# Quadratic scores of whole query rows per key block, and a new written order of steps, in a fused attention and expert layer

## What is computed

```python
A = einsum('bchf,bshf->bhcs', q_phi, k_phi) * causal       # quadratic scores, 16 heads
y = einsum('bhcs,bshd->bchd', A, v) / (sum_s A + eps)      # "lin"
win = softmax(q k^T / sqrt(8), 64 keys back) v             # "win"
x = x + concat(lin, win) @ Wout
# expert layer: logits -> top 2 of 8 experts per token, MLP and KAN experts,
# rows gathered by token index, results scatter-added
```

## Time and profile before

| what | value |
|---|---|
| median of 3 runs | 970.09 us (969.99 to 971.36) |
| the profiled execution | 976.52 us |
| its span, first to last instruction | 974.8 us |
| mean granted TensorE clock | 0.919 of full speed |
| TensorE busy | 804.0 us (82%) |
| ScalarE busy | 535.5 us (55%) |
| GpSimd busy | 486.0 us (50%) |
| VectorE busy | 445.0 us (46%) |

### The profile page before, as it was taken

How to read it: one execution, slowest core, us unless ns; L and a number is a source line. 1 busy time by engine, 2 the same in 40 slices (tenths; PEclk the granted TensorE clock), 3 DMA queues, 4 the chain that set the end, 5 groups by cost and what they waited for, 6 DMA issues and landing times.

```text
span 974.8 us, 22796 instructions
## 1 busy us (share of the span) xinstructions
PE 804.0 (82%) x8242; PEld 610.2 (63%) x8243; DVE 445.0 (46%) x1114; ACT 535.5 (55%) x729; POOL 486.0 (50%) x657
## 2 busy tenths in 40 slices
PE   4688877867878878789785696699999999999980
PEld 2456545645655555566562474589788878987870
DVE  7525314315235243254431266347666864767250
ACT  4476645635646646467462345266676766677230
POOL 8232534443346245452446255576577777654532
PEclk9799987987989989899897598799999999999985
DMA  2312130220220401204022514253564454354123
GB/s 64 103 35 62 34 95 2 68 62 1 68 62 2 128 2 52 77 2 128 1 69 55 131 34 95 82 127 53 130 142 101 83 137 121 56 133 67 18 20 103
DMA packets 91059, 68.20 MB, mean 70 GB/s; under 512 B 42894, under 2 KB 83276, under 8 KB 89038
## 3 DMA queue, kind: packets, MB, share of 16 engines
q1 hardware_dynamic: 74014, 55.11, 19.9%
q0 software_dynamic: 16912, 11.35, 8.7%
HBM read 46.86 MB, written 21.37 MB: 70 GB/s over the span
## 4 chain that ended last, share of the span: by engine, by line
PE 58%; issue 11%; POOL 11%; ACT 8%; DVE 5%; another core or an unknown queue 4%; DMA 1%; DVEq 0%; POOLq 0%; ACTq 0%
PE pv L1562 12%; PE ring L1528 10%; PE pv L1663 10%; PE ring L1510 3%; PE ring L1497 3%; PE ring L1589 3%; ACT Pb L954 3%; PE ring L1630 2%; PE ring L1447 2%; PE ring L1616 2%; PE ring L1722 2%; PE ring L1607 2%; ACT Pb L938 2%; POOL c L693 2%
## 5 line engine op out<-in xcount | busy, mean ns | idle before, releaser
L765 POOL DMA_INDIRECT acc_d<-stack,srec x84 | 137.0, 1630 | 63.6 <-DVE stack L1126 32.2
L1663 PE MATMUL pv<-Pb,vaug 128*32 128x128 f32 (+3 forms) x2816 | 138.0, 322 | 25.1 <-issue 24.3
L1204 DVE TENSOR_REDUCE maxima<-ring 128x8 f32<-128x1024 f32 x64 | 78.4, 1225 | 162.5 <-PE ring L1589 133.6
L793 POOL TENSOR_SCALAR_AFFINE_SELECT Pb<-Pb 128x1024 f32<-128x1024 f32 x64 | 68.9, 1093 | 156.3 <-ACT Pb L938 148.7
L944 ACT ACTIVATE Pb<-ring 128x768 f32<-128x768 f32 x128 | 99.6, 812 | 77.9 <-PE ring L1616 69.5
L1138 DVE SCALAR_TENSOR_TENSOR stack<-stack 128x512 f32<-128x512 f32 x160 | 104.3, 691 | 71.0 <-ACT stack L917 55.0
L1663 PEld LDWEIGHTS pv<-Pb,vaug 128*32 128x32 f32 x2816 | 82.8, 110 | 70.6 <-issue 56.3
L1528 PE MATMUL ring<-stack 128*128 128x256 f32 x560 | 124.1, 381 | 0.0
L1528 PEld LDWEIGHTS ring<-stack 128*128 128x128 f32 x560 | 105.4, 190 | 18.5 <-issue 4.7
L822 POOL DMA_INDIRECT slot_d<-rec,pos x64 | 62.4, 975 | 96.6 <-DVE pos L1305 79.5
L917 ACT ACTIVATE stack<-ring,kprm 128x512 f32<-128x512 f32 x160 | 108.2, 814 | 0.1
(11 more groups left out here) (246 smaller groups left out, 1297.0 us busy)
## 6 DMA issues: line engine op xcount, KB each, us to landing
stack<-L_ffn_kan_sl_W SPq DMA_DIRECT2D x20, 1024.0 KB
stack<-hl_d SPq DMA_DIRECT2D x24, 256.0 KB
stack<-hl_d SPq DMA_DIRECT2D x24, 128.0 KB
stack<-L_ffn_mlp_W SPq DMA_DIRECT2D x12, 256.0 KB
hl_d<-hi SPq DMA_DIRECT2D x7, 384.0 KB, 2.6
hl_d<-lo SPq DMA_DIRECT2D x7, 384.0 KB, 4.0
Pb<-L_ffn_mlp_W SPq DMA_DIRECT2D x10, 256.0 KB
xb<-L_attn_x SPq DMA_DIRECT2D x9, 256.0 KB
```

The costliest lines, as they stand in the source:

```text
L765: pool.indirect_dma_start(acc_d, bass.IndirectOffsetOnAxis(ap=srec[:, kind, u % RECS, q, 0:1], axis=0), src[:, u % 2, q, :], None, compute ...
L1204: dve.tensor_reduce(maxima[:, c, 2 * HG * n:2 * HG * (n + 1)].rearrange("p (k j) -> p k j", j=HG), slot(job).rearrange("p k (j q) -> p k j ...
L1663: mm = pe.matmul(pv[32 * j:32 * (j + 1), n // 2 % 2, q0:q0 + w], vaug[:, p, c, head(n, j) // 2, 16 * (n % 2):16 * (n % 2) + 32], src[:, j, ...
```

## The change

Scores: a pass is now 5 jobs of 1024 columns. Job 0 takes key block 2 of all four heads (256 query columns each). Jobs 1 to 4 take one head each: key block 0 with all 512 query columns, block 1 with 384, block 3 with 128. The diagonal blocks thus lie inside longer rows. GpSimd's select becomes four of 512 columns with strides (one after job 0, one after job 2, two after job 4), and the product's wait counts all four. The product takes each key block in one group: 4 groups of 4 matmuls, of 512, 384, 256 and 128 columns. Window scores are as before.

Order: the string `ORDER` is replaced. The front's statistics and coefficients come at the batch's start, `q`, `k`, `u` and `stacks` in its first third, `weights` and with it the scatter's data earlier, `mT` after `store` instead of before, `*egather` after the scatter instead of before.

```diff
--- before.py
+++ after.py
@@ -72,16 +72,16 @@
 ORDER = """
-M L L M -ytr L L M L -ycT L M -out L L L M -coef2 L L +stats M +aggr P +coef L L L L M L M L -h2norm P L +hT
--h2T L -logit L +q L +k mT L L -store P L *eload -choose W W W +u +v -rank P -total W *egather +stacks
-+residual W -gapexp W W P W Y W W -weights +xload P W W W W W W P -scatter P
+L L +stats +aggr +coef -ytr L M L L M -ycT M M -out L -coef2 +hT L M +q L +k L +u L -h2norm M P L +stacks L L L
+P L -h2T M L M -store L -logit mT L L L P -choose -rank -gapexp W W W P -weights -total +residual W W Y W W P
+*eload W W W W P W W W W +xload P -scatter W *egather +v P
 """.split()
 
 
 def batch_steps(u, tail, front):
 
 
-    series = {"L": iter([("lin", n, j, u) for n in range(NHG) for j in range(6)]),
+    series = {"L": iter([("lin", n, j, u) for n in range(NHG) for j in range(5)]),
               "M": iter([("max", n, j, u) for n in range(NHG // 2) for j in range(NT)]),
               "W": iter([("win", n, j, u) for n in range(NHG, 2 * NHG) for j in range(NT)]),
               "P": iter([("pv", n, 0, u) for n in range(2 * NHG)]),
@@ -782,16 +782,25 @@
                     if c < 5:
                         pool.wait_ge(k_cf, tile_no(k, 6, c + 1))
 
+            def own_blocks(pd):
+
+                pool.affine_select(pd, pd, [[0, HG], [1, P]], ALU.is_ge, 0.0, base=0,
+                                   channel_multiplier=-1).then_inc(pd_ready, 1)
+
             def batches():
                 for s, n, j, b in PROGRAM:
-                    if s == "lin" and j < 2:
+                    if s == "lin" and j in (0, 2, 4):
                         job = JOBS[(s, n, j, b)]
                         pool.wait_ge(freed[job % SLOTS], fill_no(job))
                         pool.sem_inc(pool_at, 1)
 
-                        pd = Pb[:, n % 2, 1024 * j:1024 * (j + 1)].rearrange("p (a q) -> p a q", q=P)
-                        pool.affine_select(pd, pd, [[0, 8], [1, P]], ALU.is_ge, 0.0, base=0,
-                                           channel_multiplier=-1).then_inc(pd_ready, 1)
+                        if j == 0:
+                            own_blocks(Pb[:, n % 2, 4 * 1024:5 * 1024].rearrange("p (j q) -> p j q", j=HG)[:, :, 0:P])
+                        else:
+                            own_blocks(Pb[:, n % 2, 1024 * (j - 2):1024 * j].rearrange(
+                                "p (j q) -> p j q", j=HG)[:, :, 0:P])
+                        if j == 4:
+                            own_blocks(Pb[:, n % 2, 0:4 * 1024].rearrange("p (j q) -> p j q", j=HG)[:, :, 1024 - P:])
                     if s == "coef":
                         front_coefficients(b + 1)
                         normed()
@@ -929,21 +938,15 @@
                         act.activation(mT16[:], slot(job)[0:H, 0, :], ACT.Copy, scale=-1.0).then_inc(mT_ready, 1)
                         act.wait_ge(mT_ready, batch_no(b, 1, 1))
                         act.sem_inc(freed[job % SLOTS], 1)
-                    if s == "lin" and j < 2:
+                    if s == "lin":
                         job = JOBS[(s, n, j, b)]
                         wait_filled(act, job)
                         if j == 0:
 
                             act.wait_ge(pv_done, batch_no(b, 8, LEAD + max(n - 1, 0)))
-                        act.activation(Pb[:, n % 2, 1024 * j:1024 * (j + 1)].rearrange("p (k q) -> p k q", k=2),
+                        at = 1024 * (j - 1 if j else HG)
+                        act.activation(Pb[:, n % 2, at:at + 1024].rearrange("p (k q) -> p k q", k=2),
                                        slot(job), ACT.Square, bias=1.0).then_inc(freed[job % SLOTS], 1)
-                    if s == "lin" and j >= 2:
-                        hd = j - 2
-                        job = JOBS[(s, n, j, b)]
-                        wait_filled(act, job)
-                        act.activation(Pb[:, n % 2, 2048 + 768 * hd:2048 + 768 * (hd + 1)].rearrange(
-                            "p (k q) -> p k q", k=2), slot(job)[:, :, 0:384], ACT.Square,
-                            bias=1.0).then_inc(freed[job % SLOTS], 1)
                     if s == "win":
                         c = j
                         job = JOBS[(s, n, c, b)]
@@ -1598,24 +1601,15 @@
                         for c in range(NT):
                             mm = pe.transpose(slot(job)[0:H, 0, P * c:P * (c + 1)], maxima[:, c, :], identf[:])
                         mm.then_inc(filled[job % SLOTS], 1)
-                    if s == "lin" and j < 2:
+                    if s == "lin":
                         job = JOBS[(s, n, j, b)]
                         wait_freed(pe, job)
-                        for bk in range(2):
-                            c = 2 * j + bk
-                            for hd in range(HG):
-                                mm = pe.matmul(slot(job)[:, bk, P * hd:P * (hd + 1)],
-                                               sk[:, head(n, hd), P * c:P * (c + 1)],
-                                               su[:, head(n, hd), P * c:P * (c + 1)], start=True, stop=True)
-                        mm.then_inc(filled[job % SLOTS], 1)
-                    if s == "lin" and j >= 2:
-                        job = JOBS[(s, n, j, b)]
-                        wait_freed(pe, job)
-                        for bk, o, c in ((0, 0, 0), (1, 0, 1), (1, 256, 2)):
-                            w = T - P * (c + 1)
-                            mm = pe.matmul(slot(job)[:, bk, o:o + w],
-                                           sk[:, head(n, j - 2), P * c:P * (c + 1)],
-                                           su[:, head(n, j - 2), P * (c + 1):T], start=True, stop=True)
+                        parts = ([(hd, 2, hd // 2, 2 * P * (hd % 2)) for hd in range(HG)] if j == 0 else
+                                 [(j - 1, 0, 0, 0), (j - 1, 1, 1, 0), (j - 1, 3, 1, T - P)])
+                        for hd, c, bk, o in parts:
+                            w = T - P * c
+                            mm = pe.matmul(slot(job)[:, bk, o:o + w], sk[:, head(n, hd), P * c:P * (c + 1)],
+                                           su[:, head(n, hd), P * c:T], start=True, stop=True)
                         mm.then_inc(filled[job % SLOTS], 1)
                     if s == "win":
                         if n == NHG and j == 0:
@@ -1634,9 +1628,9 @@
                     if s == "pv":
 
                         if n < NHG:
-                            pe.wait_ge(pd_ready, batch_no(b, 8, 2 * n + 2))
-
-                            po_job = JOBS[("lin", n, 5, b)]
+                            pe.wait_ge(pd_ready, batch_no(b, 16, 4 * n + 4))
+
+                            po_job = JOBS[("lin", n, 4, b)]
                             pe.wait_ge(freed[po_job % SLOTS], fill_no(po_job))
                         else:
 
@@ -1645,25 +1639,20 @@
                         if n % 2 == 0:
                             pe.wait_ge(y_out[n // 2 % 2], batch_no(b, 2, LEAD + n // 4))
                         for c in range(NT):
-                            parts = []
                             if n < NHG:
-                                pd = Pb[:, n % 2, 512 * c:512 * (c + 1)].rearrange("p (j q) -> p j q", j=HG)
-                                po = Pb[:, n % 2, 2048:5120].rearrange("p (j q) -> p j q", j=HG)
-                                parts.append((P * c, P, pd))
-                                if c < NT - 1:
-                                    o = (0, 384, 640)[c]
-                                    w = T - P * (c + 1)
-                                    parts.append((P * (c + 1), w, po[:, :, o:o + w]))
+                                w = T - P * c
+                                src = (Pb[:, n % 2, 4 * 1024:5 * 1024] if c == 2 else
+                                       Pb[:, n % 2, 0:4 * 1024]).rearrange("p (j q) -> p j q", j=HG)
+                                o = (0, T, 0, 1024 - P)[c]
                             else:
-                                wq = WQ if c < NT - 1 else P
-                                pw = Pb[:, n % 2, 768 * c:768 * (c + 1)].rearrange("p (j q) -> p j q", j=HG)
-                                parts.append((P * c, wq, pw[:, :, 0:wq]))
-                            for x_, (q0, w, src) in enumerate(parts):
-                                for j in range(HG):
-                                    mm = pe.matmul(pv[32 * j:32 * (j + 1), n // 2 % 2, q0:q0 + w],
-                                                   vaug[:, p, c, head(n, j) // 2, 16 * (n % 2):16 * (n % 2) + 32],
-                                                   src[:, j, :], start=(n % 2 == 0 and c == 0 and x_ == 0), stop=(c == NT - 1),
-                                                   skip_group_check=True)
+                                w = WQ if c < NT - 1 else P
+                                src = Pb[:, n % 2, 768 * c:768 * (c + 1)].rearrange("p (j q) -> p j q", j=HG)
+                                o = 0
+                            for j in range(HG):
```

(4 more changed lines are left out.)

## The result

| | before | after |
|---|---|---|
| median | 970.73 us (969.99 to 972.31, 4 runs) | 932.58 us (927.93 to 940.73, 4 runs) |
| span of the profiled execution | 974.8 us | 938.9 us |
| mean granted TensorE clock | 0.919 | 0.923 |
| TensorE busy | 804.0 us | 790.3 us |

The ratio is 0.9622, 95% interval 0.9586 to 0.9657: 38 us less, where I had forecast 14.5 less and a range down to 939. The profiled executions (976.5 and 940.7 us) both lie above their medians; spans are compared with spans.

The account below looks back on a forecast made before the run. TensorE was taken to bound each batch up to pv7, with the scatter stretch the largest loss. Terms -2.2 - 2.4 - 4.8 + 1.4 + 3.5 - 6 - 4 = -14.5 us gave 956 us from 970.1, range 939 to 977.

Parts of the forecast that it names:

- merging and hand-overs: Scores and product: wider matmuls save 2.2 us over 32 passes, one slot hand-over less per pass saves 2.4 us.
- `hT` for `hn`: TensorE's 0.79 us wait for GpSimd's normalised rows in six batches goes, as coefficients start with the batch: -4.8 us.
- opening of the batch: From pv7 to `out`, 1.4 us of idle instead of 1.2, as `ytr` stands behind fewer score jobs: +1.4 us.
- mixing of the jobs (at nothing): New alternation of score jobs with other jobs: given no term of its own in the sum, so 0 us.
- `mT` behind the stores: On SyncE's queue `mT` travels behind 0.77 MB of stores and win4.0 waits for it: +0.5 x 7 = +3.5 us.
- scatter: Scatter starts 8 to 10 us earlier, its instruction shortage falling on less dense window jobs: -1 x 6 = -6 us.
- last batch: Gather, scatter and second gather run without GpSimd's 5.28 us break and start earlier: -4 us (-9 to +8).
- Order, the front: Moved start-of-batch jobs: -4.8 us for the `hn` wait, +1.4 us for the opening; `q`, `k`, `u` alternate with score jobs.
- It is made up by the product behind them: `q`, `k`, `u` alternating with score jobs take ScalarE 0.92 + 0.6, TensorE 0.43 + 0.9 us; no net charge.
- The 81 ns rule: About 81 ns per 128-column matmul, not 56: 16 diagonal matmuls would save 13 us, giving 945; 2 in 100.
- rival (1): Scatter hits working engines, so pauses of about 7 us strike more often: slower, at about 977 us; 16 in 100.
- (4): Scatter's shortage overlaps ScalarE's backlog (-24 not -6) without pauses, or last batch yields 9: 938 to 946 us; 22 in 100.

## Why the prediction was wrong

The direction was right; the forecast of 956 us was 23 us too slow. Most of the gain lies in a term that I had as small waits taken away one by one, and the saving that I had put on the scatter did not come.

| step | predicted, us | measured |
|---|---|---|
| merging and hand-overs | -4.6 | -2.17 a batch under the new order (six: -12.4), +1.0 at full clock under the old |
| `hT` for `hn` | -4.8 | the wait is gone (0.78 a batch); with the new scores the early coefficients are worth 2.4 a batch, 5.2 with the clock |
| opening of the batch | +1.4 | no cost: pv7 to `out` 8.80 for 9.65, with 8.80 - 8.05 = 0.75 us of idle where I had found 1.4 |
| mixing of the jobs (at nothing) | 0 | the whole order is -3.5 a batch with the old scores (six: -20.5), 0.8 of it `hn` |
| `mT` behind the stores | +3.5 | 0.0 (48.26 against 48.27) |
| scatter | -6 | no saving: 11.5 for 11.0 a batch, within what single traces differ; 1.5 a batch dearer early than late on the other kind of chip |
| last batch | -4 | -0.9 |

- **The step that failed** is "Order, the front". I read 4.7 us of small waits in the earlier trace rows and took away only 0.8 a batch for `hn` and 0.3 for a hand-over. I looked at each moved word for what it adds and not at what its new place does to the jobs around it: a projection between two score jobs is also 0.9 us in which ScalarE catches up. "It is made up by the product behind them" had it as a cost that is repaid; it was part of the gain. What the runs showed in its place: TensorE's waits for ScalarE fall from 3.5 to 1.3 us a batch with the order alone and to 0.5 with the merge, and the order takes 3.5 us off the period with the old scores, 6.7 with the new. The clean period fell by 5.7 us, of which my terms without scatter and last batch (-4.5 us over the kernel) hold 0.6.
- **The merge** was priced right for TensorE's columns: a pass of scores is 1.06 + 2 x 0.82 = 2.70 us before and 0.61 + 2 x 1.04 = 2.69 after, and the product of all four blocks takes 2.36 us in 32 records (16 matmuls) against 2.38 in 56 (28 matmuls). What it saves comes with one job, one slot and one square less, and only where TensorE doesn't wait for something else. I had 0.57 us a batch for both, and it is 2.2 under the new order. That the same change costs under the old order I did not see, since I priced the four selects at nothing on GpSimd's queue. What is behind them in that queue is `hn`.
- **The 81 ns rule** (the Trainium skill, "TensorE: Matmul & The Clock Gate", section "Back-to-back issue gap") would have put the forecast nearer, for a wrong reason: the rows just given show no saving of matmuls as such.
- **The scatter.** I modelled a supply of instructions that runs short where matmuls are dense. The gaps of 1 us did move with the scatter into the window jobs, as forecast. But ScalarE, idle in it before, is now in the chain, and it pauses too (3.03 and 4.34 us), with TensorE waiting 2.46 us behind it: rival (1) in a mild form. That this is what ate my 1 us is read from the traces; no run took the pauses away by themselves.
- **What was to be seen.** pv7 to `out` under 12 us at full clock (8.80), no wait for `hn` from the first `out` on, product groups of 2.36 us with 32 records: right. No long pauses: wrong. `mT` was waited for once, 0.80 us. The product waited for GpSimd's select at 0.3 to 0.6 us a few times, not 1.2.
- **The rivals.** (4), the larger gain, came nearest, but only by its end of 938, which is still too slow, and not by its cause. I had taken scatter and last batch for the uncertain part. For the clean batch no rival said that the new mixing could save several times the waits I had listed one by one, and that is what happened.

## What to carry to other kernels

Judge a written order in a version with the noisy operation left out: most of its periods repeat to 0.1 to 0.4 us and tell parts apart that full runs blur. Price a moved step by what it does between its new neighbours: here jobs whose consumer (ScalarE, 0.8 to 1.0 us) is slower than their producer (TensorE, 0.5 to 0.6 us) gained by a job of another consumer behind every one or two. And a part that loses alone (here the merged scores, by their selects ahead of `hn`) can pay beside another, so both orders of applying them have to be measured.

## What the runs showed of the hardware

- The same kernel took 970 us on one kind of chip and 885 to 887 on four others, with clean periods alike. The difference lies in the batches with GpSimd's indirect transfers, 10.4 to 11.5 us each on the one kind, 0 to 2.8 in the kernels traced on the other.
- A wait of 2.63 us was followed by 8.4 us at a granted clock of 0.59 in five batches of six, which cost 2.8 to 3.0 us on top. In the sixth the same wait left the clock at 1.00.
- A busy GpSimd without indirect transfers (24 selects, 11.13 us a batch) cost 0.8 us over six periods; eight such transfers, in a run or singly, cost 13.0 and 12.8. The pauses of ScalarE have no releaser in the trace, and what it waits for stays open.
- Runs of 8 and 16 f16 matmuls of 128 columns took 0.61 and 1.06 us, 56 ns for a further one, and joining them into wider ones left a pass of scores at 2.69 us of TensorE for 2.70.
